# s spread over the partition groups by two-pass float32 products on 32-row tiles instead of a rounded part and a rest, in a block of layer norm, small attention and feed-forward

## The reference

```python
s = jnp.einsum('btd,dm->btm', x, Win) + bin_          # 512 -> 64
h = jax.nn.relu(s[..., None] * W1 + b1)               # 64 -> 64 x 16
g = jnp.einsum('btmh,mh->btm', h, W2) + b2            # 64 x 16 -> 64
out = jnp.einsum('btm,md->btd', g, Wout) + bout       # 64 -> 512
```

## Time and profile before

| | us |
|---|---|
| three runs | 314.58, 319.86, 320.58 |
| median | 319.86 |
| span of the profiled execution | 312.5 |
| PE busy | 279.0 (89%) |
| DVE busy | 259.3 (83%) |
| POOL busy | 241.0 (77%) |
| ACT busy | 232.5 (74%) |

### The profile page before, as it was taken

The page is one execution under the profiler, slowest core; times in us unless marked ns, Lnnn a source line. Parts: engine busy times, 40 slices in busy tenths (PEclk is TensorE's granted clock), DMA queues, the critical chain, the costliest instruction groups (busy, mean ns, idle before and its releaser), DMA issues.

```text
span 312.5 us, 6071 instructions
## 1 busy us (share of the span) xinstructions
PE 279.0 (89%) x2287; PEld 123.2 (39%) x2287; DVE 259.3 (83%) x400; ACT 232.5 (74%) x282; POOL 241.0 (77%) x209
## 2 busy tenths in 40 slices
PE   4988899889979789899998989898989898989982
PEld 4844645335333353334433343333332434342220
DVE  0759759799799969998889999999998998965544
ACT  1548673758987789859998784879787979797840
POOL 8440999693949959978889793979797979799920
PEclk9999999999999999999999999999999999999998
DMA  7999969988359699798998999699999999551697
GB/s 243 286 367 362 269 181 356 423 211 278 96 172 330 206 271 335 217 356 257 288 266 252 364 289 381 195 339 321 303 351 340 366 354 335 191 229 42 214 339 271
DMA packets 50572, 87.86 MB, mean 281 GB/s; under 512 B 6360, under 2 KB 35184, under 8 KB 46448
## 3 DMA queue, kind: packets, MB, share of 16 engines
q1 hardware_dynamic: 46400, 65.96, 66.6%
q10 hardware_dynamic: 3504, 21.37, 19.6%
q0 software_dynamic: 640, 0.16, 0.8%
HBM read 53.77 MB, written 33.69 MB: 280 GB/s over the span
## 4 chain that ended last, share of the span: by engine, by line
PE 41%; DVE 29%; issue 10%; DMA 8%; ACT 7%; POOL 3%; ACTq 1%; DVEq 0%; POOLq 0%
PE TA L514 10%; PE g L582 10%; DVE stats L1145 8%; DVE x L1118 8%; PE op L619 6%; DMA out_dram<-x 5%; ACT xT L820 3%; DMA b2c<-in_L_ffn_b_dram 3%; PE TA L481 3%; ACT H L845 3%; PE rep L566 2%; PE TA L619 2%; DVE xqT L1128 2%; DVE SL L1139 2%; PE A L328 1%
## 5 line engine op out<-in xcount | busy, mean ns | idle before, releaser
L1272 POOL TENSOR_TENSOR x<-x,bias_row 128x512 f32<-128x512 f32 x128 | 167.7, 1347 | 0.0
L845 ACT ACTIVATE H<-rep,b1c,w1c 128x1024 f32<-128x1024 f32 x124 | 144.4, 1206 | 24.2 <-PE rep L566 21.9
L1145 DVE BATCH_NORM_STATS2 stats<-x 128x6 f32<-128x512 f32 x128 | 78.6, 676 | 8.9 <-DMA x<-in_L_attn_x_dram 8.9
L1118 DVE TENSOR_TENSOR x<-x,op 128x1024 f32<-128x1024 f32 x46 | 55.4, 1204 | 14.7 <-PE op L619 14.5
L582 PE MATMUL g<-H,w2s 128*32 128x512 f32 x512 | 62.6, 599 | 0.4 <-ACT H L845 0.4
L1256 POOL TENSOR_TENSOR rstd<-veps,nhalf 128x8 f32<-128x8 f32 x16 | 26.4, 1648 | 33.5 <-DVE veps L1155 33.3
L619 PE MATMUL op<-wout,G 64*128 64x512 f32 x184 | 49.9, 620 | 1.2 <-ACT G L852 0.8
L514 PE MATMUL TA<-xT,win 128*32 128x512 f32 x208 | 47.0, 593 | 0.3 <-ACT s_full L825 0.3
L514 PE MATMUL TA<-xqT,winq 128*32 128x512 f32 x208 | 47.0, 593 | 0.0
L1128 DVE STREAM_TRANSPOSE xqT<-xq 128x1024 f32<-128x1024 f32 x28 | 34.6, 1236 | 0.8 <-DMA xq<-in_L_attn_x_dram 0.8
L820 ACT ACTIVATE xT<-TA 128x1024 f32<-128x1024 f32 x26 | 26.7, 1025 | 8.2 <-PE TA L481 7.7
(11 more groups left out here) (190 smaller groups left out, 361.9 us busy)
## 6 DMA issues: line engine op xcount, KB each, us to landing
out_dram<-x SPq DMA_DIRECT2D x30, 1024.0 KB, 6.9
x<-in_L_attn_x_dram ACTq DMA_DIRECT2D x10, 2048.0 KB, 11.2
xq<-in_L_attn_x_dram SPq DMA_DIRECT2D x112, 128.0 KB, 7.7
x<-in_L_attn_x_dram SPq DMA_DIRECT2D x12, 1024.0 KB, 10.8
out_dram<-x SPq DMA_DIRECT2D x4, 512.0 KB, 3.3
x<-in_L_attn_Wq_dram SPq DMA_DIRECT2D x1, 1024.0 KB, 17.9
x<-in_L_attn_Wk_dram SPq DMA_DIRECT2D x1, 1024.0 KB, 20.0
x<-in_L_attn_Wv_dram SPq DMA_DIRECT2D x1, 1024.0 KB, 7.7
```

Source lines behind the costliest of these rows:

```text
L845: act.activation(Hr[half][k % len(Hr[half])][:, :], rep_banks(n, half)[:, :], ACT.Relu, bias=b1c[:, half, k:k + 1], scale=w1c[:, half, k:k ...
L1118: dve.tensor_tensor(both, both, sum_banks(n, j)[:, :].rearrange("p (h d) -> p h d", h=2), ALU.add).then_inc(add_done, 1)
L1145: dve.bn_stats(stats[:, j, :], x_sb[m][:, j * D:(j + 1) * D]).then_inc(bn_done, 1)
L1272: pool.tensor_tensor(x_sb[m][:, c], x_sb[m][:, c], bias_row[:, :], ALU.add).then_inc(xc_done, 1)
```

## The change

The float32r copies SH and SL go, with their two steps and semaphores. `spread` becomes one float32 matrix of 128 x 128 whose rows of every group of 32 partitions spread that group. The product for one half of s reads 32 rows of s_full directly, on tiles of 32 rows and 128 columns, in float32. 1/std is copied into a buffer of its own, R_sb, and `scale_s` writes s_full, for which it now waits until both products of the block before have read it. Lines of the schedule by hand lose their s_high and s_low and are otherwise as they were.

```diff
-        SH, SL = sb("SH", [P, BLK], F32R), sb("SL", [P, BLK], F32R)
+        R_sb = sb("R", [P, BLK])
...
-        spread = sb("spread", [P, 2, P], F32R)
+        spread = sb("spread", [P, P])
...
         def replicate(n, half):
...
             if half == 0:
-                pe.wait_ge(sl_done, n + 1)
+                pe.wait_ge(s_done, n + 1)
...
-            for part in (SH, SL):
-                for b in range(2):
-                    own = slice(b * M, (b + 1) * M)
-                    mm = pe.matmul(rep_banks(n, half)[:, b * BLK:(b + 1) * BLK], spread[own, half, :], part[own, :], start=(part is SH), stop=(part is SL),
-                                   tile_position=(b * M, 0))
+            for b in range(2):
+                row0 = b * M + half * MH
+                own = slice(row0, row0 + MH)
+                mm = pe.matmul(rep_banks(n, half)[:, b * BLK:(b + 1) * BLK], spread[own, :], s_full[own, :],
+                               start=True, stop=True, tile_position=(row0, 0))
             mm.then_inc(rep_done, 1)
...
         def copy_rstd_late(n):
             act.wait_ge(rb_done, n + 1)
-            act.wait_ge(sl_done, n)
-            act.activation(s_full[:, :].rearrange("p (h x) -> p h x", h=2), half_banks[:, :, 0, :], ACT.Copy).then_inc(R_done, 1)
-
-        def s_high(n):
-            act.wait_ge(s_done, n + 1)
-            if n > 0:
-                act.wait_ge(rep_done, 2 * n)
-            act.activation(SH[:, :], s_full[:, :], ACT.Copy).then_inc(sh_done, 1)
+            act.wait_ge(s_done, n)
+            act.activation(R_sb[:, :].rearrange("p (h x) -> p h x", h=2), half_banks[:, :, 0, :], ACT.Copy).then_inc(R_done, 1)
...
-            for half in range(2):
-                ins = dve.tensor_copy(spread[:, half, :].rearrange("p (g m) -> p g m", g=HG),
-                                      isum[:, half * MH:(half + 1) * MH].unsqueeze(1).to_broadcast([P, HG, MH]))
-            ins.then_inc(spread_made, 1)
+            dve.wait_ge(dve_own, v)
+            dve.tensor_copy(spread[:, :].rearrange("p (g m) -> p g m", g=HG),
+                            istack[:, :].unsqueeze(1).to_broadcast([P, HG, MH])).then_inc(spread_made, 1)
...
         def scale_s(n):
             dve.wait_ge(sc_done, 4 * n + 4)
             dve.wait_ge(R_done, n + 1)
-            dve.tensor_tensor(s_full[:, :], s_ps[:, :], s_full[:, :], ALU.mult).then_inc(s_done, 1)
-
-        def s_low(n):
-            dve.wait_ge(sh_done, n + 1)
             if n > 0:
                 dve.wait_ge(rep_done, 2 * n)
-            dve.tensor_tensor(SL[:, :], s_full[:, :], SH[:, :].bitcast(F32), ALU.subtract).then_inc(sl_done, 1)
+            dve.tensor_tensor(s_full[:, :], s_ps[:, :], R_sb[:, :], ALU.mult).then_inc(s_done, 1)
```

More of the change, by code:

```diff
@@ L158, in residual_block @@
         rb_done, R_done, s_done = sem("rb_done"), sem("R_done"), sem("s_done")
-        sh_done, sl_done, rep_done = sem("sh_done"), sem("sl_done"), sem("rep_done")
+        rep_done = sem("rep_done")
         relu_done, g_done = sem("relu_done"), sem("g_done")
@@ L813, in copy_rstd @@
             if n > 0:
-                act.wait_ge(sl_done, n)
-            act.activation(s_full[:, :], g_ps[:, :], ACT.Copy).then_inc(R_done, 1)
+                act.wait_ge(s_done, n)
+            act.activation(R_sb[:, :], g_ps[:, :], ACT.Copy).then_inc(R_done, 1)
         def evacuate_late(n, i):
@@ L865, in act_program @@
                 evacuate(n, 0)
-                if n == 1:
-                    s_high(0)
                 reach(side, n, 0)
@@ L886, in act_program @@
                 reach(side, n, 6)
-                if n > 1:
-                    s_high(n - 1)
                 if n + AHEAD >= RING and has(n + AHEAD):
@@ L943, in act_program @@
             relu(N - 2, 4)
-            s_high(LAST)
             relu(N - 2, 5)
@@ L1164, in dve_program @@
                     scale_s(0)
-                    s_low(0)
                 turn_quads(n, 0)
@@ L1184, in dve_program @@
                 reach(side, n, 6)
-                if n > 1:
-                    s_low(n - 1)
                 reach(side, n, 7)
@@ L1226, in dve_program @@
             add(N - 3, 0)
-            s_low(LAST)
             add(N - 3, 1)
```

## The result

| | before | after |
|---|---|---|
| median of the runs | 317.22 us (313.79 to 320.58) | 320.71 us (320.63 to 321.04) |
| ratio, 95% interval | | 1.0215 (1.0193 to 1.0236) |
| profiled span | 312.5 us | 318.9 us |

The executions of the kernel before fall into two groups, 313 to 315 us and from 317.7 us up, and every ratio here leaves out, of both kernels, the executions more than 1.5% above the fastest, so nearly all of the second group. The changed kernel is about 2% slower: that it is slower is clear, and 2% lies inside the interval. Its span grew by 6.4 us, where +7.5 was forecast.

The account below looks back on a forecast made before the run. DVE was taken as nearly full beside the attention, a PE-ACT circle of waits as the late blocks' bound. Terms -0.75 + 3.2 + 3.65 + 1.4 = +7.5 us on the 319.86 us median gave 327.4 us, range 318.5 to 332.

Parts of the forecast that it names:

- rival (a): From 61 to 209 us DVE is binding and its relief carries whole: +0.9 us in all, 320.7 us; chance 0.28.
- The bound now: Late blocks, from 209 us: no engine is full; a circle of waits between PE and ACT holds them at about 14.8 us.
- The product: Each of 32 float32 spreading products runs 1.13 us, reaches its reader 0.40 us later and holds PE 0.39 us longer.
- The new shape: Changing to 32-row tiles and back costs 0.20 us after a block's second product, 0.09 us at the first.
- Rival (b): Changes of tile shape cost the full 0.2 us on both sides: +14 us, 334 us; chance 0.12.
- The new wait: s_full can start only 1.13 + 0.04 us after the product starts, and ends just ahead of the second projection.
- Late blocks: Five blocks, 209 to 283 us: 0.83 us each, 4.15, less 0.5 cover from one block's store wait: +3.65 us.
- Attention blocks: Eight blocks, 61 to 209 us: +0.9, +0.5, +1.1 and +0.7 us, nothing in four: +3.2, bounds -2 and +6.
- Start: Around 45.83 to 59.47 us, SH and SL gone win 1.1 us, the added wait takes back 0.35: -0.75 us.
- End: From 283.46 us: three products on the chain of waits, one at 0.40 and two at 0.48 us: +1.4 us.
- Rival (c): DMA queues set the pace, slower compute only fills their time: late blocks +0.3, total +4, 323.9 us; chance 0.13.
- From span to median: Whole kernel: the median's distance of 7.4 us above the profiled span was kept, taking 320.0 us to 327.4 us.

Follow-up runs that it names:

- f32_rows64_two_s: The changed kernel with the spreading product on tiles of 64 rows and two buffers for s_full, so without the added wait: 316.49 us, ratio 1.0076 to before.
- twice_passes: The kernel before with each pair of spreading products (SH, SL) made twice, no new shape or wait: 320.87 us, ratio 1.0223.
- f32_two_s: The changed kernel with two buffers for s_full, so its scaling no longer waits for the products of the block before: 321.95 us, ratio 1.0214 to before.
- onepass_rows64: The changed kernel with s_full rounded to float32r and spread in a single pass on 64-row tiles, low bits lost, wait kept: 311.75 us, ratio 0.9891 to before.
- one-pass kernels: Two variants of the changed kernel with a single-pass rounded product on 64-row tiles, with one or two s_full buffers: 311.75 and 310.09 us, ratios 0.9891 and 0.9873.

## Why the prediction was right, and where its sizes were off

The forecast was 327.4 us, 318.5 to 332, with the line between the same and slower inside it; the measured median is 320.7 and the ratio 1.0215. That is inside the range, but outside the 324.5 to 331 that the text gave to its own mechanism, and exactly at the 320.7 of rival (a), whose mechanism the trace refutes. That the range held is in part luck: its lower end was there for (a). What the trace bears out is the mechanism and the growth of the span, 6.4 us against 7.5.

- **The bound now, a circle of PE and ACT in the late blocks:** right in that PE's product lengthens it: in f32_rows64_two_s the second product's 0.39 us are the block's 0.40. But "ACT's saving buys nothing in the late blocks" holds only beside the short pair. With long products the four relus end late, and twice_passes shows that SH would then hold the next first product and relu 0 behind it. SH and SL gone hide the first product's extra length, 0.3 us or more a block. The sum had this part right: it let the first product start without a wait for SL.
- **The product, 1.13 us, PE held 0.39 longer:** right to 0.01, read from the projection's rows. In f32_rows64_two_s it holds PE 0.96 us, 0.39 more than the pair.
- **The new shape, 0.09 in and 0.11 more for the projection behind:** right (1.05 from product to projection at 241.02, projection of 1.13). Taken away with the wait gone, it gives 0.35 us a block, about the 0.29 of the sum; with the wait there, 0.15, since the second projection then exposes its weights either way. Rival (b), dear shapes, did not come.
- **The new wait:** s_full starts 1.27 us after the product (1.17 forecast) and ends "just ahead of the second projection", as said. What was missed is that just ahead isn't enough: the projection loads its weights only when released, 0.10 us more, and the turn likewise behind a late addition. That is the mis-sized term of a late block, 0.95 instead of 0.83.
- **Late blocks, +3.65:** measured +4.6. Three cost 0.95, the block with the store wait 0.47 (15.24 to 15.71; the cover of 0.5 is there), and the last one 1.3 (16.06): there the first product comes 6.94 us after the second of the block before and not 6.59, in both profiles of the changed kernel. The rows of that block show DVE's queue behind the late s_full there: its turn (275.15) starts after 0.27 us idle, the third projection (277.56) comes only when the first addition is done (277.50), the turn (278.73) when the second is (278.63). f32_two_s, without the wait, keeps to 6.38 us there as in its other blocks.
- **Attention blocks, +3.2:** measured +2.6 in the trace. The place at 81 us is as forecast, in the changed kernel's rows:

```profile
80.37 1.13 PE L566 MATMUL rep<-s_full,spread 32*128 32x512 f32 x4
...
81.64 0.69 DVE L1122 TENSOR_TENSOR s_full<-TA,R 128x512 f32<-128x512 f32 x1 [3.48 <-PE rep L566]
```

DVE, which idled 1.64 us ahead of s_full in the earlier trace rows, now idles 3.48, and near 175 us it idles 0.95 where it had not idled at all. Rival (a), DVE's relief carrying, was refuted for this product. With a cheap one, in onepass_rows64, these blocks came out at -1.6 us, near the -2 of the lower bound, but its product is 0.23 us shorter than the pair, so not by the relief alone.
- **Start, -0.75:** measured -1.2 once the 0.94 of the loads is taken off. SL at 45.83 and its wait are gone, and the new wait took nothing back, where 0.35 was assumed: from the first product to the fourth it is 35.0 us in the changed kernel and in f32_two_s, which has no such wait.
- **End, +1.4:** measured +1.4.
- **Rival (c), the DMA queues:** not here, but near. It is what holds up the one-pass kernels' late blocks, by the timeline shown.
- **From span to median:** the failed step. The sum gave 320.0 for the span and the trace 318.9. To it were added the 7.4 us by which the median of three runs lay above the profiled span. But two of those three were executions of the long group, of which the changed kernel, without SL, shows none in 8. Above its span the changed kernel's median lies 1.8 us. With the fastest run's distance, 2.1, which the text also gave, the same sum is 322.1 us. So 5.6 of the 6.7 us of error come from this step and 1.1 from the sum.

## What to carry to other kernels

Count what an edit adds to the engine that releases the others, with every change of tile shape and every weight load that a later release lays bare, before counting what it takes from engines with idle time: here 27.7 us less of DVE and ACT work weighed less than some 0.4 us on PE in each of 32 products, and what its shape and its wait add. A wait that costs 0.2 to 0.4 us a block where the queue behind it is short costs 0.7 where another operation of the chain stands in it, so measure a wait with the queue that it will have. And where the runs of one kernel fall into groups, don't carry the median over to a changed kernel: look first for an operation whose duration can make the gap, and whether the edit removes it.

## What the runs showed of the hardware that was not expected

A DVE operation with both inputs in SBUF (SL, 128x512) takes 0.67 to 1.66 us in most places, but 6.16, 6.16 and 6.57 us in three profiled executions, each time beginning amid a gapless run of POOL additions (15, 15 and 14 of them) and ending 0.54 to 0.56 us after the last. In other executions it got through such a run in 1.24 and 1.65 us. WvT, too, with both inputs in SBUF, took 0.67 to 0.71 us in some places and up to 1.84 beside the additions. s_full, whose one input is in PSUM, was never held (0.67 to 0.69 us in all profiles read for it). The Trainium skill has a rule of this kind (SBUF — State Buffer, "SBUF: two separate sides"): DVE and GpSimd share a pair of SBUF ports under an exclusive lock, which a DVE operation with two SBUF inputs needs against a GpSimd operation that reads SBUF, for the whole instruction, and the loser is blocked. The traces agree as to which operations are hit, and the 6 us are those of an operation that waits until POOL is done. But if the rule is read so that the loser goes next, an SL would lose at most the rest of one addition, some 1.27 us (19.0 for 15), and so come to the 1.24 to 1.65 that most show; that it can lose to every addition of a run, the rule doesn't say and three traces here show. What decides between the two stays open.

Each such hold costs more than its own length. PE was idle for 4.83, 4.84 and 4.61 us, and the granted clock, which fell to 1.2 GHz meanwhile, stayed there for some 3 to 5 us with PE at work again.

A float32 product of 128 columns by 512 takes 1.13 us whether its tile has 64 rows or 32. With 64 the projection behind it, on the same shape, starts 0.96 us later; with 32 it starts 1.05 later, across a change of shape.
